# A residual adapter stack on one Trainium2 core: two batches quantised in halves, and additions moved into accumulating DMAs

## The chip, the cores and the metric

The kernel runs on one core of a Trainium2 chip. A core has five engines that run side by side and wait for each other through semaphores: TensorE (PE; PEld is its weight load), VectorE (DVE), ScalarE (ACT), GpSimd (POOL) and SyncE (SP), which here only issues transfers. The metric is the device time of one execution in microseconds; lower is better.

## The reference

`x` has 8 batches of 256 tokens with 1024 features, in float32. Four residual steps follow each other:

```
x1 = x + quantise(x; 8 thresholds, deltas, zero points)
x2 = x1 + x1 @ W1[a_b].T                 # a_b: adapter of batch b, 1024 x 1024
x3 = x2 + x2 @ W2.T + 0.5 * (x2 @ A[l_b]) @ B2.T      # rank 32
x4 = x3 + (x3 @ B3[a_b].T) @ A3[a_b].T                # rank 16
```

`quantise` counts for each element how many of the 8 thresholds are at least its absolute value; the count picks delta and zero point; x/delta is rounded, shifted, clipped to 0..63 and dequantised. Where all eight thresholds hold (the count is 8) the result is 0.

## The kernel before

All work lies transposed: 128 features in the partitions, `KT` = 8 such blocks, and `T` = 256 tokens in the columns, so a batch is a tile of 128 x 2048. `G` = 8 groups.

*Quantising.* Each batch takes 8 steps, numbered `n` from 0 over all batches (`STEPS` = 64). For a step ScalarE computes `multiple(n)` (x/delta plus a rounding constant, into the ring `tq` of 3) and `exceeds(n)` (a mask, ring of 2). VectorE computes `value(n)`, `clamp(n)` and `select(n)` (a predicated copy into `y`). At the end `close_batch` cuts and adds: `x1 = x + y`, written into `xs`, and raises `x1_ready`. Other work of the two engines is written into this sequence at fixed steps: `ACT_G` and `ACT_E` (steps at which ScalarE copies adapter tables G and E out of PSUM), `ACT_W2` and `DVE_W2` (W2's eight rows), and, counted from a batch's end, `X2_AT`, `V_AT`, `U_AT`, `LOW_AT`, `OUT_AT`.

*W1.* TensorE computes x2 = (W1 + I) x1 in float32 (`w1_x1`, two matmul passes, 64 products of 256 columns a batch). The identity is added to W1's diagonal blocks by GpSimd (`w1_diagonal`), in pairs `j` = 0 to 3 of output blocks.

*W2.* The product is made in three terms of a shorter format: x2 is split in `x2h` (ScalarE, `round_x2`) and `x2l` (VectorE, `split_x2`), W2 + I in `w2h` (ScalarE) and `w2l` (VectorE, a subtract), and `product` adds x2h w2h, x2l w2h and x2h w2l. A W2 row (128 x 1024) comes into one of `ST` = 4 stage buffers; GpSimd adds the identity (`w2_diagonal`); a buffer is loaded again when `w2l` of its row is done. Buffer 0 is `ua`, which later holds the adapter's U. W2 is prepared once and stays.

*Adapters.* Before batch 0 TensorE makes the tables G and E (`bilinear`, `adapters_g`, `adapters_e`), which go through DRAM. `v_x2` and `u_low` add the low-rank part to the accumulators.

*Order.* TensorE: adapter tables, then for each batch W1 (for batches above 0 with the `u_low` of the batch before in it), then W2 with `v_x2`. SyncE's queue, in order: first x (in two halves), tables, W1 and W2 rows as TensorE finishes G, then x of batch 1, E's stores, the other W2 rows, `load_u`; then in each batch the next W1 in four pairs, V, x of the batch after the next, and U.

Of the kernel before, what the change touches and what calls it, by code (L numbers as in the profile page):

```python
# [5 lines left out]
def quantised_residual_adapter_stack(nc, x, params, w1, w2t, w2n, b3t, b2n, b2r, a3, la, ids_b, ids_a,  # L6
# [12 lines left out]
    P = 128  # L19
# [12 lines left out]
    CP = CH // 2  # L32
# [6 lines left out]
    STEPS = B * G  # L39
# [3 lines left out]
    TQ, MK, ST = 3, 2, 4  # L43

    ctx = ExitStack()
    with ctx:
# [85 lines left out]
        w1_ready = sem("w1_ready")  # L132
# [3 lines left out]
        w2_diag = sem("w2_diag")  # L136
# [16 lines left out]
        w2l_ready = sem("w2l_ready")  # L153
# [16 lines left out]
        def _(sp):  # L170
# [69 lines left out]
            sp.wait_ge(w2l_ready, ST + 1)  # L240
# [30 lines left out]
        def _(pool):  # L271
# [39 lines left out]
        def _(act):  # L311
            def multiple(n):
                c, g = n // G, group_of(n)
                if n == 0:
                    for h in range(2):
                        act.wait_ge(x_first[h], 16)
                        nc.scalar.activation(tq[:, 0, h * CP:(h + 1) * CP], flat(xs[:, 0, h * HALF:(h + 1) * HALF, :]),
                                             ACT.Identity, bias=magic[:, 0:1], scale=rdelta[:, g:g + 1]) \
                            .then_inc(t_ready, 1)
                    return  # L320
                if n % G == 0:
                    act.wait_ge(x_in[c % 2], 16 * ((c + 1) // 2 if c % 2 else c // 2))
                if n >= TQ:
                    act.wait_ge(chosen, n - TQ + 1)
                nc.scalar.activation(tq[:, n % TQ, :], flat(xs[:, c % 2, :, :]), ACT.Identity, bias=magic[:, 0:1],  # L325
                                     scale=rdelta[:, g:g + 1]).then_inc(t_ready, 1)

            def absolute(c):
                act.wait_ge(y_cut, c)
                nc.scalar.activation(absx[:, :], flat(xs[:, c % 2, :, :]), ACT.Abs).then_inc(abs_ready, 1)  # L330

            def exceeds(n):
                if n % G:
                    act.wait_ge(abs_ready, n // G + 2)
# [5 lines left out]
                    nc.scalar.activation(mask[:, n % MK, :], absx[:, :], ACT.Relu,  # L340
# [42 lines left out]
            def tables(n):  # L383
# [19 lines left out]
            for n in range(END):  # L403
# [10 lines left out]
                for b in range(B):  # L414
                    s = n - G * (b + 1)
                    if s == V_AT + 1:
                        round_v(b)
                    for q in range(ACCS):
                        if s == OUT_AT[q] + 1 and b < LAST:
                            finish_out(b, q)  # L420
                    if s == U_AT:
                        round_u(b, 0)
                        round_u(b, 1)
                    for h, at in enumerate(X2_AT if b else X2_FIRST):
                        if s == min(at + 2, G - 1):
                            round_x2(b, h)
                    if s == LOW_AT + 1:
# [6 lines left out]
        def _(dve):  # L434
            def value(n):
                g = group_of(n)
                dve.wait_ge(t_ready, n + 2)
                nc.vector.tensor_scalar(tq[:, n % TQ, :], tq[:, n % TQ, :], -MAGIC, par[:, 1, g:g + 1],  # L438
                                        ALU.add, ALU.mult).then_inc(u_ready, 1)

            def first_value(h):
                g = group_of(0)
                dve.wait_ge(t_ready, h + 1)
                half = tq[:, 0, h * CP:(h + 1) * CP]
                nc.vector.tensor_scalar(half, half, -MAGIC, par[:, 1, g:g + 1], ALU.add, ALU.mult).then_inc(u_ready, 1)
# [12 lines left out]

            def select(n):
# [286 lines left out]
```

## Time and profile before

| | before |
|---|---|
| median of 3 runs | 491.61 us (489.53 to 491.75) |
| profiled execution, its own time | 492.2 us |
| its span | 490.4 us |
| PE busy | 457.0 us (93%) |
| DVE busy | 391.1 us (80%) |
| ACT busy | 319.7 us (65%) |
| POOL busy | 68.1 us (14%) |
| mean share of the 16 DMA engines | 36.6% |

The span runs from the first to the last instruction of the profiled execution; its own time is what the device measured for it, with what lies around the span. Busy shares are averages over stages that differ. A matmul in float32 appears as two records.

### The profile page before, as it was taken

How to read it: one execution, taken by the hardware profiler on the slowest of the kernel's cores; microseconds unless marked ns; L12 is line 12 of the kernel's file. 1: busy time of each engine (PE TensorE's matmuls, PEld its weight loads, DVE VectorE, ACT ScalarE, POOL GpSimd, SP SyncE). 2: the span in 40 equal slices, each digit the busy share in tenths (PEclk: the TensorE clock that was granted, in tenths of full speed). 3: DMA queues.
4: the chain of work that ended last, by engine and by line, in shares of the span. 5: the costliest groups of instructions: out<-in, count | busy, mean ns of one | idle time of the engine just before them, and what ended most of it. 6: DMA issues, size and time to landing. Idle time of an engine off the chain costs nothing.

```text
span 490.4 us, 5532 instructions
## 1 busy us (share of the span) xinstructions
PE 457.0 (93%) x2160; PEld 391.8 (80%) x2160; DVE 391.1 (80%) x267; ACT 319.7 (65%) x240; POOL 68.1 (14%) x46
## 2 busy tenths in 40 slices
PE   1992399997999999999999999999999999999997
PEld 1980388886888888888888888888888888888885
DVE  4997999999999999999699959995999969300100
ACT  5957899739984995697839884797569782104001
POOL 1072060380012004300020002000210002000000
PEclk9997599999999999999999999999999999999999
DMA  8997151740185018500760047201850074102002
GB/s 281 365 347 273 52 172 33 285 188 4 44 319 200 0 44 315 204 0 16 269 247 31 0 147 303 111 0 43 315 203 0 13 275 158 32 0 87 0 1 86
DMA packets 16818, 67.03 MB, mean 137 GB/s; under 512 B 2464, under 2 KB 5792, under 8 KB 11808
## 3 DMA queue, kind: packets, MB, share of 16 engines
q1 hardware_dynamic: 16800, 66.81, 36.6%
q8 instruction: 9, 0.15, 0.1%
q14 instruction: 9, 0.07, 0.0%
HBM read 56.84 MB, written 9.96 MB: 136 GB/s over the span
## 4 chain that ended last, share of the span: by engine, by line
PE 82%; DVE 11%; ACT 2%; issue 2%; DMA 1%; SPq 1%; DVEq 0%; ACTq 0%
PE x2p L610 39%; PE acc L635 31%; DVE y L463 5%; PE acc L585 3%; PE x2p L621 3%; DVE tq L451 2%; PE acc L645 2%; DVE tq L438 2%; PE acc L647 2%; DMA rows<-own_rows 1%; DVE y L471 1%; ACT tq L325 1%; ACT mask L340 1%; PE acc L573 1%; DVE w2l L511 1%
## 5 line engine op out<-in xcount | busy, mean ns | idle before, releaser
L610 PE MATMUL x2p<-xs,w1b 128*128 128x256 f32 x1024 | 225.4, 381 | 19.9 <-DVE xs L474 19.9
L610 PEld LDWEIGHTS x2p<-xs,w1b 128*128 128x128 f32 x1024 | 195.5, 191 | 48.3 <-DVE xs L474 17.8
L325 ACT ACTIVATE tq<-xs,magic,rdelta 128x2048 f32<-128x2048 f32 x63 | 131.2, 2094 | 39.0 <-DMA xs<-x 34.2
L463 DVE COPY_PREDICATED y<-mask,tq 128x2048 f32<-128x2048 int16 x56 | 143.2, 2556 | 1.9 <-ACT mask L340 0.7
L340 ACT ACTIVATE mask<-absx,negtop 128x2048 bf16<-128x2048 f32 x56 | 111.5, 1993 | 0.4 <-DVE y L463 0.4
L284 POOL TENSOR_TENSOR w1b<-w1b,eye 128x256 f32<-128x256 f32 x32 | 53.5, 1676 | 321.3 <-DMA w1b<-w 321.3
L438 DVE TENSOR_SCALAR tq<-tq,par 128x2048 f32<-128x2048 f32 x63 | 81.6, 1304 | 2.4 <-ACT tq L325 2.4
L635 PE MATMUL acc<-w2h,x2h 128*128 128x512 f32 x256 | 81.3, 396 | 0.0
L451 DVE TENSOR_SCALAR tq<-tq,ylow,yhigh 128x2048 f32<-128x2048 f32 x56 | 80.7, 1441 | 0.0
L635 PE MATMUL acc<-w2h,x2l 128*128 128x512 f32 x256 | 79.6, 390 | 0.0
L635 PE MATMUL acc<-w2l,x2h 128*128 128x512 f32 x256 | 79.5, 389 | 0.0
L479 DVE TENSOR_TENSOR x2l<-x2p,x2h 128x1024 fp32r<-128x1024 f32 x16 | 19.5, 1220 | 55.4 <-ACT x2h L345 55.4
L635 PEld LDWEIGHTS acc<-w2h,x2l 128*128 128x128 f32 x256 | 48.1, 188 | 10.2
L635 PEld LDWEIGHTS acc<-w2l,x2h 128*128 128x128 f32 x256 | 48.0, 188 | 10.2
L635 PEld LDWEIGHTS acc<-w2h,x2h 128*128 128x128 f32 x256 | 47.5, 188 | 9.4 <-DVE x2l L479 0.3
L345 ACT ACTIVATE x2h<-x2p 128x1024 fp32r<-128x1024 f32 x16 | 16.4, 1026 | 42.8 <-PE x2p L610 42.8
L381 ACT ACTIVATE outb<-acc 128x512 f32<-128x512 f32 x32 | 17.3, 593 | 37.3 <-PE acc L647 37.3
L371 ACT ACTIVATE low_hc<-x2p,lscale 128x256 fp32r<-128x256 f32 x8 | 3.8, 471 | 31.5 <-PE x2p L621 31.5
L471 DVE SCALAR_TENSOR_TENSOR y<-absx,top,y 128x2048 f32<-128x2048 f32 x8 | 19.2, 2397 | 0.3
L474 DVE TENSOR_TENSOR xs<-xs,y 128x2048 f32<-128x2048 f32 x8 | 18.3, 2292 | 0.3
L495 DVE SCALAR_TENSOR_TENSOR low_lh<-x2p,lscale,low_hc 64x256 fp32r<-64x256 f32 x8 | 3.7, 468 | 17.6 <-ACT low_lh L373 17.6
L585 PE MATMUL acc<-xs,w1b 128*128 128x128 f32 x128 | 17.7, 297 | 0.0
(59 smaller groups left out, 249.2 us busy)
## 6 DMA issues: line engine op xcount, KB each, us to landing
w1b<-w SPq DMA_DIRECT2D x32, 1024.0 KB, 6.6
xs<-x SPq DMA_DIRECT2D x7, 1024.0 KB, 6.8
out<-outb SPq DMA_DIRECT2D x14, 512.0 KB, 2.8
w1b<-w2n SPq DMA_DIRECT2D x4, 1024.0 KB, 11.3
ring<-w2t SPq DMA_DIRECT2D x6, 512.0 KB, 6.2
ua<-e_dram SPq DMA_DIRECT2D x16, 128.0 KB, 2.5
xs<-x SPq DMA_DIRECT2D x2, 512.0 KB, 5.4
ua<-w2t SPq DMA_DIRECT2D x2, 512.0 KB, 4.5
```

The source lines that it names most:

```text
L284: nc.gpsimd.tensor_tensor(diag, diag, eye[:, :].unsqueeze(1).to_broadcast([P, 2, P]), ALU.add) \
L325: nc.scalar.activation(tq[:, n % TQ, :], flat(xs[:, c % 2, :, :]), ACT.Identity, bias=magic[:, 0:1], scale=rdelta[:, g:g + 1]).then_inc(t_ ...
L340: nc.scalar.activation(mask[:, n % MK, :], absx[:, :], ACT.Relu, bias=negtop[:, g:g + 1], scale=1.0).then_inc(mask_ready, 1)
L438: nc.vector.tensor_scalar(tq[:, n % TQ, :], tq[:, n % TQ, :], -MAGIC, par[:, 1, g:g + 1], ALU.add, ALU.mult).then_inc(u_ready, 1)
L451: nc.vector.tensor_scalar(tq[:, n % TQ, :], tq[:, n % TQ, :], ylow[:, g:g + 1], yhigh[:, g:g + 1], ALU.max, ALU.min).then_inc(clamped, 1)
L463: nc.vector.copy_predicated(y[:, :], mask[:, n % MK, :].bitcast(i16), tq[:, n % TQ, :]) \
L471: nc.vector.scalar_tensor_tensor(y[:, :], absx[:, :], top[:, G - 1:G], y[:, :], ALU.is_gt, ALU.mult).then_inc(y_cut, 1)
L474: nc.vector.tensor_tensor(xc, xc, y[:, :], ALU.add).then_inc(x1_ready, 1)
L479: nc.vector.tensor_tensor(flat(x2l[:, half, :]), x2p[:, 2 * i:2 * i + 2, :].rearrange("p j n -> p (j n)"), flat(x2h[:, half, :]).bitcast(f ...
L585: last = nc.tensor.matmul(into, w2g[:, i, o * P:(o + 1) * P], b3s[:, o, :], start=False, stop=(o == OT - 1))
L610: last = nc.tensor.matmul(x2p[:, o // 2, o % 2 * T:(o % 2 + 1) * T], w1b[:, o, at:at + P], xs[:, slot, k, :], start=(o % 2 == 0 and k == 0 ...
L635: nc.tensor.matmul(acc[2 * t + h][:, :], xp[:, k, cut], w[:, k, h * DH:(h + 1) * DH], start=(k == 0 and xp is x2h and w is w2h), stop=Fals ...
```

## The change

Batches 0 and 1 are quantised as four "chains" of 1024 columns (features 0 to 511 and 512 to 1023 of each), batches 2 to 7 as one chain of 2048 each, so there are 10 chains and 80 steps. The helper names take `width(n)` and `x_part(c)` for sizes and places; `close_batch` becomes `close_chain`. TensorE multiplies the first two batches by W1 in two parts: first the products with blocks 0 to 3 of x1 for the outputs, then those with blocks 4 to 7. For batch 0 the W2 product does all terms with `w2h` first (`HIGH`), then `v_x2`, then the term with `w2l` (`LOW`).

The identities are no longer added by a GpSimd operation but by a DMA that GpSimd issues and that adds to its destination. `w2l` is no longer subtracted by VectorE: ScalarE writes the negated `w2h` into `w2l`, and a DMA of GpSimd's adds the row to it. There are five stage buffers instead of four. The steps for the other work are set anew. TensorE's loop over batches begins with batch 2.

```diff
+    CHAINS = [(b, lo, lo + HALF) for b in range(2) for lo in (0, HALF)] + [(b, 0, KT) for b in range(2, B)]
+    STEPS = len(CHAINS) * G
-    TQ, MK, ST = 3, 2, 4
+    TQ, MK, ST = 3, 2, 5
...
+        def chain_after(b):
+            return 2 * (b + 1) if b < 1 else b + 3
+        def w2l_count(k):
+            return 16 * (k // ST + 1)
...
             def load_w2(k):
                 if k >= ST:
-                    sp.wait_ge(w2l_ready, k - ST + 1)
+                    sp.wait_ge(w2l_ready[k % ST], w2l_count(k - ST))
...
                 load_w2(j)
+            load_w2(PAIRS)
...
-            sp.wait_ge(w2l_ready, ST + 1)
+            sp.wait_ge(w2l_ready[0], w2l_count(ST))
             load_u(a0)
...
-                nc.gpsimd.tensor_tensor(diag, diag, eye[:, :], ALU.add).then_inc(w2_diag, 1)
+                pool.dma_start(diag, eye[:, :], accum_op=ALU.add).then_inc(w2_diag[k % ST], 16)
+            def w2_remainder(k):
+                pool.wait_ge(w2n_ready, k + 1)
+                pool.dma_start(w2l[:, k, :].bitcast(f32), stage[k % ST], accum_op=ALU.add) \
+                    .then_inc(w2l_ready[k % ST], 16)
...
-                nc.gpsimd.tensor_tensor(diag, diag, eye[:, :].unsqueeze(1).to_broadcast([P, 2, P]), ALU.add) \
-                    .then_inc(w1_ready, 1)
+                pool.dma_start(diag, eye[:, :].unsqueeze(1).to_broadcast([P, 2, P]), accum_op=ALU.add) \
+                    .then_inc(w1_ready[j], 16)
             for j in range(PAIRS):
                 w1_diagonal(0, j)
                 w2_diagonal(j)
-            for k in range(PAIRS, KT):
+            for k in range(PAIRS, ST):
                 w2_diagonal(k)
-            with pool.Fori(1, B) as b:
+            for k in range(ST):
+                w2_remainder(k)
+            for k in range(ST, KT):
+                w2_diagonal(k)
+            for k in range(ST, KT):
+                w2_remainder(k)
+            for b in range(1, B):
...
-        DVE_D = 2
-        ACT_G, ACT_E = 5, 6
-        ACT_W2 = (9, 9, 10, 10, 12, 13, 13, 14)
-        DVE_W2 = (8, 8, 9, 9, 11, 12, 12, 13)
-        X2_FIRST, X2_AT = (2, 5), (4, G - 1)
-        V_AT, U_AT = 3, G - 1
-        LOW_AT = G + 1
-        OUT_AT = (G + 4, G + 4, G + 5, G + 5)
+        DVE_D = 4
+        ACT_G, ACT_E = 10, 12
+        ACT_W2 = (13, 13, 14, 14, 15, 25, 25, 26)
+        X2_AT = [(4, 6), (3, 5)] + [(4, G - 1)] * (B - 2)
+        V_AT = [7] + [3] * (B - 1)
+        U_AT = [13] + [G - 1] * (B - 1)
+        LOW_AT = [14] + [G + 1] * (B - 1)
+        OUT_AT = [(17, 17, 18, 18)] + [(G + 4, G + 4, G + 5, G + 5)] * (B - 1)
...
-                    act.wait_ge(w2_diag, k + 1)
+                    act.wait_ge(w2_diag[k % ST], 16 * (k // ST + 1))
                     nc.scalar.activation(w2h[:, k, :], stage[k % ST], ACT.Copy).then_inc(w2h_ready, 1)
+                    nc.scalar.activation(w2l[:, k, :], stage[k % ST], ACT.Copy, scale=-1.0).then_inc(w2n_ready, 1)
...
-                    dve.wait_ge(w2h_ready, k + 1)
-                    nc.vector.tensor_tensor(w2l[:, k, :], stage[k % ST], w2h[:, k, :].bitcast(f32),
-                                            ALU.subtract).then_inc(w2l_ready, 1)
...
+            HIGH, LOW = ((x2h, w2h), (x2l, w2h)), ((x2h, w2l),)
...
+            FRONT, BACK = range(HALF), range(HALF, KT)
+            def first_batch():
+                pe.wait_ge(x1_ready, 1)
+                w1_x1(0, 0, range(OT), first=True, parts=FRONT)
+                pe.wait_ge(x1_ready, 2)
+                w1_x1(0, 0, range(OT), parts=BACK)
+                pe.wait_ge(g_ready, 2)
+                for i, ks in enumerate((FRONT, BACK)):
+                    pe.wait_ge(x2l_ready, i + 1)
+                    for t in range(UN):
+                        for k in ks:
+                            if t == 0:
+                                pe.wait_ge(w2h_ready, k + 1)
+                            product(t, k, HIGH)
+                pe.wait_ge(vl_ready, 2)
+                v_x2()
+                for t in range(UN):
+                    for k in range(KT):
+                        if t == 0:
+                            pe.wait_ge(w2l_ready[k % ST], w2l_count(k))
+                        product(t, k, LOW)
+            def second_batch():
+                pe.wait_ge(x1_ready, 3)
+                w1_x1(1, 1, range(OT - 2), parts=FRONT)
+                pe.wait_ge(lowl_ready, 1)
+                w1_x1(1, 1, range(OT - 2, OT), parts=FRONT)
+                for q in range(ACCS):
+                    u_low(0, q)
+                pe.wait_ge(x1_ready, 4)
+                w1_x1(1, 1, range(OT), parts=BACK)
+                w2_x2(1)
```

## Rows read from the trace of the kernel before

**Rows 1.** The page, part 4: shares of the chain that ended last, by engine.
```profile
PE 82%; DVE 11%; ACT 2%; issue 2%; DMA 1%; SPq 1%; DVEq 0%; ACTq 0%
```

**Rows 2.** The chain in order of time: start us, us, what.
```profile
125.41 17.27 PE x2p L610 x80
142.68 16.37 PE acc L635 x72
159.04 1.89 PE x2p L621 x16
...
166.40 10.36 PE x2p L610 x48
```

**Rows 3.** Timeline of PE: start us, us, engine, line, operation [idle before it, releaser].
```profile
38.58 1.02 PE L598 MATMUL x2p<-outb,dmask 128*128 128x512 f32 x2
56.60 29.61 PE L610 MATMUL x2p<-xs,w1b 128*128 128x256 f32 x128 [17.00 <-DVE xs L474]
...
112.92 10.62 PE L610 MATMUL x2p<-xs,w1b 128*128 128x256 f32 x48 [2.85 <-DVE xs L474]
```

**Rows 4.** Windows of PE: stretch, us, busy (x), granted clock, DMA share, GB/s.
```profile
42.00:44.00 2.00, 0.00 (x0) 0.76 0.15 31
...
60.00:62.00 2.00, 2.00 (x10) 0.97 0.00 0
```

**Rows 5.** Timeline of DVE.
```profile
33.86 1.75 DVE L451 TENSOR_SCALAR tq<-tq,ylow,yhigh 128x2048 f32<-128x2048 f32 x1
...
121.56 1.34 DVE L451 TENSOR_SCALAR tq<-tq,ylow,yhigh 128x2048 f32<-128x2048 f32 x1
122.81 1.28 DVE L438 TENSOR_SCALAR tq<-tq,par 128x2048 f32<-128x2048 f32 x1
124.01 2.50 DVE L463 COPY_PREDICATED y<-mask,tq 128x2048 f32<-128x2048 int16 x1
126.41 1.32 DVE L451 TENSOR_SCALAR tq<-tq,ylow,yhigh 128x2048 f32<-128x2048 f32 x1
...
158.06 2.29 DVE L474 TENSOR_TENSOR xs<-xs,y 128x2048 f32<-128x2048 f32 x1
...
205.46 2.29 DVE L474 TENSOR_TENSOR xs<-xs,y 128x2048 f32<-128x2048 f32 x1
```

**Rows 6.** Groups by form, DVE: line, shapes, count, busy us, mean ns, idle before.
```profile
L463 DVE COPY_PREDICATED y<-mask,tq 128x2048 f32<-128x2048 int16 x56 | 143.2, 2556 | 1.9 <-ACT mask L340 0.7 <-issue 0.4
...
L474 DVE TENSOR_TENSOR xs<-xs,y 128x2048 f32<-128x2048 f32 x8 | 18.3, 2292 | 0.3
...
L511 DVE TENSOR_TENSOR w2l<-ring,w2h 128x1024 fp32r<-128x1024 f32 x6 | 7.2, 1224 | 0.0
...
L445 DVE TENSOR_SCALAR tq<-tq,par 128x1024 f32<-128x1024 f32 x2 | 1.4, 748 | 0.0
```

**Rows 7.** Groups by form, ACT, same columns.
```profile
L394 ACT ACTIVATE w2h<-ring 128x1024 fp32r<-128x1024 f32 x6 | 6.1, 1041 | 0.0
...
L317 ACT ACTIVATE tq<-xs,magic,rdelta 128x1024 f32<-128x1024 f32 x2 | 2.5, 1240 | 1.8 <-DMA xs<-x 1.6 <-DVE yhigh L524 0.3
```

**Rows 8.** Timeline of ACT at the E copies.
```profile
39.63 1.09 ACT L398 ACTIVATE outb<-acc 128x512 f32<-128x512 f32 x2 [1.91 <-PE x2p L598]
```

**Rows 9.** Page part 6 (count, KB each, us to landing); timelines of SP and ACT.
```profile
out<-outb SPq DMA_DIRECT2D x14, 512.0 KB, 2.8
w1b<-w2n SPq DMA_DIRECT2D x4, 1024.0 KB, 11.3
ring<-w2t SPq DMA_DIRECT2D x6, 512.0 KB, 6.2
...
91.41 0.45 SPq L172 DMA_DIRECT2D xs<-x  x1
...
105.00 4.10 ACT L325 ACTIVATE tq<-xs,magic,rdelta 128x2048 f32<-128x2048 f32 x2 [8.22 <-DMA xs<-x]
```

**Rows 10.** One line, GpSimd's W1 diagonal: ns min/median/max, first and last start.
```profile
L284 POOL TENSOR_TENSOR w1b<-w1b,eye x32: 726/1157/6553, 25.9 to 413.4; 128x256 f32<-128x256 f32 x32
```

More of the change, by code:

```diff
@@ L131, in quantised_residual_adapter_stack @@
         x1_ready = sem("x1_ready")
-        w1_ready = sem("w1_ready")
+        w1_ready = [sem(f"w1_ready{j}") for j in range(PAIRS)]
         w1_used = sem("w1_used")
@@ L135, in quantised_residual_adapter_stack @@
         out_ready = sem("out_ready")
-        w2_diag = sem("w2_diag")
+        w2_diag = [sem(f"w2_diag{c}") for c in range(ST)]
+        w2n_ready = sem("w2n_ready")
         x2h_ready = sem("x2h_ready")
@@ L152, in quantised_residual_adapter_stack @@
         w2h_ready = sem("w2h_ready")
-        w2l_ready = sem("w2l_ready")
+        w2l_ready = [sem(f"w2l_ready{c}") for c in range(ST)]
         block = ctx.enter_context(nc.Block())
@@ L545, in _ @@
                         value(n + 1)
-                for b in range(B):
-                    if n == G * (b + 1) + G - 1 and X2_AT[1] == G - 1 and b:
+                for b in range(1, B):
+                    if n - G * chain_after(b) == G - 1 == X2_AT[b][1]:
                         split_x2(b, 1)
@@ L599, in adapters_e, with w1_x1 @@
                                      a3s[:, cols], start=False, stop=True).then_inc(e_done, 1)
-            def w1_x1(b, slot, tiles, first=False):
+            def w1_x1(b, slot, tiles, first=False, parts=range(KT)):
                 for o in tiles:
-                    if o % 2 == 0:
-                        pe.wait_ge(w1_ready, PAIRS * b + o // 2 + 1)
-                    if first and o == HALF:
+                    if o % 2 == 0 and parts[0] == 0:
+                        pe.wait_ge(w1_ready[o // 2], 16 * (b + 1))
+                    if first and o == HALF and parts[0] == 0:
                         pe.wait_ge(e_ready, 2 * EH)
-                    for k in range(KT):
+                    for k in parts:
                         at = (k - o) % KT * P
@@ L613, in w1_x1 @@
                                                 skip_group_check=True)
-                    if o % 2 == 1:
+                    if o % 2 == 1 and parts[-1] == KT - 1:
                         last.then_inc(w1_used, 1)
@@ L624, in v_x2, with product @@
                 last.then_inc(low_done, 1)
-            def product(b, t, k, first=False, halves=(0, 1)):
+            HIGH, LOW = ((x2h, w2h), (x2l, w2h)), ((x2h, w2l),)
+            def product(t, k, terms=HIGH + LOW, halves=(0, 1)):
                 cut = slice(t * P, (t + 1) * P)
-                for xp, w in ((x2h, w2h), (x2l, w2h), (x2h, w2l)):
-                    if first and t == 0 and xp is x2h:
-                        if w is w2h:
-                            pe.wait_ge(w2h_ready, k + 1)
-                        else:
-                            pe.wait_ge(w2l_ready, k + 1)
+                for xp, w in terms:
                     for h in halves:
@@ L650, in _ @@
             LOW_TILES = 3
-            def batch(b, slot, first=False, last=False):
-                pe.wait_ge(x1_ready, b + 1)
-                if first:
-                    w1_x1(b, slot, range(OT), first=True)
-                    pe.wait_ge(g_ready, 2)
-                else:
-                    w1_x1(b, slot, range(LOW_TILES))
-                    for q in range(ACCS):
-                        u_low(b - 1, q)
-                    w1_x1(b, slot, range(LOW_TILES, OT))
+            FRONT, BACK = range(HALF), range(HALF, KT)
@@ new lines, in second_batch, with batch @@
+            def second_batch():
[8 more added lines that the diff above has]
+                w2_x2(1)
+            def batch(b, slot, last=False):
+                pe.wait_ge(x1_ready, b + 3)
+                w1_x1(b, slot, range(LOW_TILES))
+                for q in range(ACCS):
+                    u_low(b - 1, q)
+                w1_x1(b, slot, range(LOW_TILES, OT))
+                w2_x2(b, last)
@@ L662, in batch, with w2_x2 @@
+            def w2_x2(b, last=False):
                 pe.wait_ge(x2l_ready, 2 * b + 1)
                 for t in range(UN):
-                    if not first:
-                        pe.wait_ge(out_ready, ACCS * (b - 1) + 2 * (t + 1))
-                    for k in range(HALF):
-                        product(b, t, k, first)
+                    pe.wait_ge(out_ready, ACCS * (b - 1) + 2 * (t + 1))
+                    for k in FRONT:
+                        product(t, k)
                 pe.wait_ge(x2l_ready, 2 * b + 2)
@@ L671, in batch @@
                     v_x2()
-                    for k in range(HALF, KT):
-                        product(b, 0, k, first)
+                    for k in BACK:
+                        product(0, k)
                     u_low(b, 0)
@@ L676, in batch @@
                     for h in range(2):
-                        for k in range(HALF, KT):
-                            product(b, 1, k, first, (h,))
+                        for k in BACK:
+                            product(1, k, halves=(h,))
                         u_low(b, 2 + h)
                 else:
-                    for k in range(HALF, KT):
-                        product(b, 0, k, first)
+                    for k in BACK:
+                        product(0, k)
                     pe.wait_ge(vl_ready, 2 * (b + 1))
                     v_x2()
-                    for k in range(HALF, KT):
-                        product(b, 1, k, first)
+                    for k in BACK:
+                        product(1, k)
             bilinear()
@@ L690, in _ @@
             adapters_e()
-            batch(0, 0, first=True)
-            with pe.Fori(0, LAST // 2) as p:
-                batch(2 * p + 1, 1)
+            first_batch()
+            second_batch()
+            with pe.Fori(0, (LAST - 2) // 2) as p:
                 batch(2 * p + 2, 0)
+                batch(2 * p + 3, 1)
+            batch(LAST - 1, (LAST - 1) % 2)
             batch(LAST, LAST % 2, last=True)
```

111 lines of the change are left out of this document (49 added, 62 removed).

## The prediction

> **What bounds the kernel now.** I began with the page's chain that ended last, then read it in order of time, then each engine's timeline up to 170 us. The reader is to see that TensorE ends everything: 82% of the chain is its own [rows 1]. From 112.92 us it runs without a gap: batch 1 takes 53.5 us (112.92 to 166.40), and each later one the same [rows 2]. What is left to win is ahead of that. TensorE idles (after the first loads) twice: 17.0 us from the end of the adapter products to the first W1 product, and 2.85 us between batches 0 and 1; both are waits for VectorE's quantised x1 [rows 3]. The first of them also costs clock: idle from 39.6 us, TensorE is granted half (1.2 of 2.4 GHz) from about 43 us (0.76 over 42 to 44), and gets full clock back some 3.5 us after work resumes at 56.6, which makes that W1 product 29.3 us instead of the later 27.6 (10.36 + 17.27) [rows 2 to 4].
>
> Behind that, VectorE is the second bound: it closes batch 0 at 56.5 and batch 1 at 112.8, just ahead of TensorE's starts [rows 3], and batch 2 at 160.3 us [rows 5]. TensorE asks for batch 2 at 166.4, so VectorE is only 6.1 us ahead there; from then on it needs 47.4 us a batch (160.3 to 207.7, [rows 5]) against 53.2, and gains 5.8 each time. So the whole change comes down to one number: when can batch 2's W1 product start? It starts at 166.40 now and needs both TensorE's end of batch 1 and the third close. Everything after is 324.0 us of gapless TensorE work (490.4 - 166.4) that the change leaves alone. The profiled execution took 492.2 us, 1.8 above its span and 0.6 above the median of 491.6; I take the change of that start off the median.
>
> **The change, part by part.**
>
> *Widths.* Batches 0 and 1 now go in four half chains of 1024 columns. VectorE's durations give a fixed part: subtract 1.22 at 1024 columns, add 2.29 at 2048; value 0.75 [rows 6] against 1.28 [rows 5]. By starts, a full step is 1.25 (clamp, 121.56 to 122.81) + 1.20 (value) + 2.40 (select) = 4.85 [rows 5]. Half a step: value 0.66 (two took 1.41), clamp 0.72 by the same halving; no half select is in the trace: 1.20 if it is exactly half; with 1.07 for 1024 columns (2.29 - 1.22) the full 2.50 has a fixed 0.36, and the half would be 1.43, by starts 1.34 to 1.43. I take 1.34, since the other operations keep their fixed part too. Step 2.72, chain 8 x 0.66 + 8 x 0.72 + 7 x 1.34 + 2.4 close = 22.9 us. Four chains cost 32 x (2.72 - 2.43) = 9.4 us more than two full batches. Removed from VectorE are eight w2l subtracts of 1.14 (1.22 less the overlap of 0.08 that the adds show) = 9.1 us [rows 6]. So VectorE wins nothing in sum. On ScalarE operations overlap by 0.1; a half multiple takes 1.24 (1.14 with the overlap), one w2 copy 1.04 (0.95) [rows 7]. The half mask lies between the two; I take 1.04. The new negated copies, of the w2 copy's shape, add 8 x 0.95 = 7.6 us.
>
> *Chains 0 and 1.* Chain 0: first value about 7.0 (x's first half is in at 5.7 and one half multiple follows), then the 22.9, dmask 0.4 and small waits: closed 30.9. TensorE is with the adapters until 39.6, as before, so this half is ready long before it. Front W1 (half of 27.6) runs 39.6 to 53.5; its W1 tiles have long been on the way (GpSimd adds the first diagonal at 25.9 [rows 10]), and pair 3 is needed only at 50. Chain 1 would be closed at 54, but ScalarE stands in the way: step 12 has the four E copies, which wait for TensorE until 39.6 (a stall that is there now [rows 8]) and end 41.75; then steps 13 and 14 carry two W2 rows each: multiple 1.14 + mask 1.04 + 4 x 0.95 = 6.0 apiece; step 15 one row, 4.1; the last mask 1.04: 41.75 + 12.0 + 4.1 + 1.05 = 58.9. The masks and tq rings are two and three deep, so VectorE waits for each. Select 1.34, close 2.4: x1's second half at 62.7. TensorE idles 9.2 us (53.5 to 62.7), and back W1 ends at 76.5; with the half clock after the idle 1.6 more, 78.1 (85.9 now).
>
> *W2 products of batch 0.* Chain 2 closes at 62.7 + 22.9 + 2.3 (two x2l) + 0.65 (v_hl) + some 1.6 of waits for ScalarE's late x2h and the like = 90.2. The x2l halves come at 77.4 and 85.1, front HIGH products (7.3 us, 32 of 0.227 [rows 2]) end at 85.4, and row 4 at 86.3. Rows 5, 6, 7 of w2h stand in ScalarE's queue at steps 25 and 26, behind the Abs that waits for chain 2's close (89.1): ready at 91.0, 92.9, 97.0. That is a new stall of 9 to 10 us on TensorE, and in 11 us it works only 2.7, so I expect the half clock again: 1.7 us. From 97.0: row 7 0.9, four of t=1 3.65, v_x2 1.9, LOW 7.3: 110.8, with the clock 112.5. It ends at 110.1 now [rows 3]. The next batch starts at once instead of at 112.92: batch 1 ends 112.5 + 53.3 = 165.8. First path.
>
> *VectorE to the third close.* Chain 3: 22.9, ScalarE's rows 5 to 7 hold it 3.6, u_hl and low_lh 1.7: 90.2 to 118.8 (TensorE wants it at 126, no wait). Batch 2 needs x(2). SP loads it after load_u(a0), which now waits for the remainder DMA of row 5: issued on GpSimd when the negated copy is done (91.9). Queued behind it on SP: four u, four W1, two v loads and x(2). The trace shows no accumulating DMA. Nearest rows: 512 KB take 2.8 (a store from SBUF) or 6.2 (a W2 load), and 1 MB in the crowd at the start 11.3 [rows 9]; I keep 2.8 and 11.3 as ends. I take 5, nearer the loads, since the queues are empty but it reads both operands: lands 97, u 2.2, W1 issues 2.5 (x(2) goes out 101.9; 91.4 now), and 13.6 to land as now (91.41 to 105.0): 115.5. ScalarE gives the first multiple at 117.7, the first mask at 125.5, and VectorE is back in step 0.7 late. Third close: 118.8 + 47.5 (112.8 to 160.3) + 0.7 - 1.5 for GpSimd operations that no longer stretch VectorE's = 165.5. Second path.
>
> *Diagonals by DMA.* In batches 1 to 7 they land perhaps 2 to 7 us later than GpSimd's add of 0.7 to 6.6; W1 loads of a later batch go out 20 us and more ahead of use, so this costs nothing; without that cover each would cost its lateness four times a batch. For batch 1, pair 0 lands about 108, wanted at 112: free too. GpSimd's own operations go; a clamp of VectorE's beside them took 1.75 instead of 1.34 [rows 5], but up to 113 us that lies mostly where VectorE will wait for ScalarE anyway. This is where a rule could speak against the change: GpSimd's 128x256 add takes 0.73 to 6.55 us [rows 10], so the two engines do hold each other up. The Trainium skill, SBUF — State Buffer, section "SBUF: two separate sides", says a DMA issued from GpSimd can't get its descriptors written while VectorE holds the shared port pair, and gives 3.1 instead of 0.62 us. By that rule (no DMA of GpSimd's is in this trace to agree or not) each issue would pay it, and the sum would be case C's below.
>
> Sum: batch 2 starts at the later of 165.8 and 165.5, plus 0.1: 165.9, against 166.4. Gain 0.5 us: 491.1.
>
> **The rivals.**
>
> *A, halves cost half (faster).* If select and mask have little fixed part, chains 2 and 3 take 2.2 us less each: w2h rows, x(2) and both paths come 2 to 3 us earlier, and if the clock is not lost 1.7 more: start 161.5 to 163.5, 486.5 to 489. For it: VectorE's fixed part at 2048 is only known from other operations. Against: the E copies pin ScalarE's pile to 39.65 us, and halves of value and multiple do keep their fixed part.
>
> *B, the remainder DMA is slow (slower).* SP's queue hangs on row 5's remainder. Every us over 5 puts x(2) and the third close back by one; it decides (over 2.5 us slower) from 8.5 us on. At 11.3, the crowded end, the third close is 171.8: 497.4. For it: read, add and write of 512 KB. Against: at 92 us the queues are empty.
>
> *C, GpSimd can't issue in time (slower).* Nine DMAs stand in its queue before the first remainder, and ScalarE's row 4 wants its diagonal at 56. From 25.9 that leaves 2.8 us an issue; if each takes 4 (inside the 0.73 to 6.55 that GpSimd's add takes beside VectorE [rows 10]), row 4 comes at 67, x1's second half and all after it 9 to 11 us later: about 500. The Trainium skill's rule in SBUF — State Buffer, above, would bring this about.
>
> *D, the full gain (faster).* TensorE's 17.0 + 2.85 idle and 1.7 us of clock all go and nothing takes their place: 21 us. I exclude it but for 0.03: VectorE was only 6.1 us ahead at the third close, so more than 6 can't be had unless its chains shrink; the cap is 485.5.
>
> **How the numbers follow.** Forecast 0.42, A 0.27, D's cap 0.03, B 0.19, C 0.09. A measurement of this kernel can tell about 0.5% (2.5 us) from no change. Faster 0.30, within 0.42, slower 0.28. Both signs hold much, so the range goes from 485.5 (cap) to 497 (B's end, C left out); the likeliest case's own range is 489.2 to 494.
>
> **What would show it.** Right: first W1 product at 39.7; a TensorE gap of about 9 us near 54 to 63, released by VectorE's x1; a gap near 86 to 97 released by ScalarE's w2h; batch 2's first product near 166; VectorE gaps for ScalarE at 40 to 60. Half selects at 1.3 to 1.4. A: half selects near 1.25, the close of chain 2 before 88. B: x(2)'s landing after 118 and ScalarE waiting for it. C: GpSimd's DMA issues of 4 us, ScalarE waiting for w2_diag before 56 us. The prediction is wrong if batch 2's first product isn't between 164 and 168.5, or if gaps open after it.

## The result, and the profile after

| | before | changed kernel |
|---|---|---|
| median | 491.21 us (4 runs) | 515.41 us (4 runs) |
| ratio to before | | 1.0484, 95% interval 1.0433 to 1.0535 |
| span of the profiled execution | 490.4 us | 512.8 us |
| batch 2's first W1 product | 166.40 us | 188.42 us |

One of the four timed executions of the changed kernel took 1684.05 us; the median counts it and the ratio leaves it out (the median of the other three is 514.54 us), and it stays unexplained.

The change is 4.8% slower. I had forecast 491.1 us, no measurable change, and 485.5 to 497 as the range. The span grew by 22.4 us and the start of batch 2 came 22.0 us later, so the loss lies where I had said that all of it would be decided, ahead of batch 2. From the page of the changed kernel come its shares of the chain that ended last and two rows of its transfers (count, KB each, us to landing). `w1b<-eye` is the DMA that adds the identity to a W1 diagonal, `w2l<-ring` the one that adds a W2 row to its negated copy (the remainder):

```profile
PE 69%; DMA 8%; DVE 8%; issue 7%; ACT 6%; SPq 2%; POOL 1%; ACTq 0%; DVEq 0%
...
w1b<-eye POOLq DMA_DIRECT2D x32, 128.0 KB, 4.1
...
w2l<-ring POOLq DMA_DIRECT2D x6, 512.0 KB, 8.3
```

TensorE had 82% of the chain [rows 1]; now transfers, and time in which no wait is shown, have taken their part. TensorE's timeline of the changed kernel, its groups with a gap before them (start, length, and in brackets the gap and its releaser):

```profile
57.86 6.44 PE L619 MATMUL x2p<-xs,w1b 128*128 128x256 f32 x16 [5.52 <-DMA w1b<-eye]
69.32 16.20 PE L619 MATMUL x2p<-xs,w1b 128*128 128x256 f32 x64 [5.02 <-DVE xs L496]
97.10 0.87 PE L641 MATMUL acc<-w2h,x2h 128*128 128x512 f32 x2 [3.37 <-ACT w2h L420]
...
126.80 16.46 PE L619 MATMUL x2p<-xs,w1b 128*128 128x256 f32 x64 [8.18 <-DMA w1b<-eye]
...
188.42 10.62 PE L619 MATMUL x2p<-xs,w1b 128*128 128x256 f32 x48 [1.64 <-DVE xs L496]
```

Against [rows 3]: the 17.0 us gap became several. The one for x1's second half is there, but it ends at 69.3 instead of my 62.7. Two gaps that I hadn't forecast wait for a W1 diagonal: pair 3 of batch 0 (5.5 us, until 57.9) and pair 0 of batch 1 (8.2 us, until 126.8). GpSimd's timeline shows what led to the first (its last row is from batch 1):

```profile
26.26 1.33 POOL L307 DMA_DIRECT2D w1b<-eye  x1 [23.68 <-DMA w1b<-w]
...
37.11 1.39 POOL L307 DMA_DIRECT2D w1b<-eye  x1 [8.58 <-issue]
...
44.84 1.39 POOL L307 DMA_DIRECT2D w1b<-eye  x1 [4.93 <-issue]
...
48.90 1.20 POOL L307 DMA_DIRECT2D w1b<-eye  x1 [1.73 <-issue]
53.73 0.91 POOL L296 DMA_DIRECT2D ring<-eye  x1 [3.63 <-issue]
58.12 0.87 POOL L296 DMA_DIRECT2D ring<-eye  x1 [3.48 <-issue]
...
127.00 1.22 POOL L307 DMA_DIRECT2D w1b<-eye  x1 [10.49 <-issue]
```

In these rows an issue itself takes 0.9 to 1.4 us. But GpSimd stands still ahead of it, "issue" being time for which the profile shows no wait: 8.6 us before pair 1, though its load had landed at 32.1. ScalarE asked for W2's rows in the meantime. Its timeline in the changed kernel:

```profile
53.48 1.06 ACT L420 ACTIVATE w2h<-ring 128x1024 fp32r<-128x1024 f32 x1 [3.74 <-DMA ring<-eye]
...
58.19 1.06 ACT L420 ACTIVATE w2h<-ring 128x1024 fp32r<-128x1024 f32 x1 [2.70 <-DMA ring<-eye]
...
143.82 1.09 ACT L407 ACTIVATE outb<-acc 128x512 f32<-128x512 f32 x2 [7.06 <-PE acc L653]
```

The first two rows are 6.4 us of waits in ScalarE's pile of copies, and x1's second half came 6.6 us later than worked out. The third comes back below. The chain in order of time shows the second transfer gap:

```profile
98.40 4.49 DMA w2l<-ua
...
103.10 0.35 SPq L201
...
105.64 1.33 SPq L212
...
107.83 0.83 SPq L213
...
110.05 4.83 DMA w1b<-w
114.88 0.44 issue
115.31 11.35 DMA w1b<-eye
126.66 0.14 issue
126.80 16.46 PE x2p L619 x64
```

The remainder of W2's row 5 lands in 4.5 us, near the 5 that I took. Then SP sends U (L201) and reads batch 1's adapter numbers (L212 and L213), and W1's pair 0 goes out only at 110.05, 7.2 us after that landing. Pair 0's diagonal, 128 KB, takes 11.4 us. It lands at 126.7, and GpSimd's next issue starts at 127.0 (the last row of its timeline).

### The profile page after: what moved, and what is told of

It is laid out like the page before. It is cut to its first block, busy times and chain, and to the rows that moved or that the text cites. A ratio compares the mean times of both kernels' runs of the same rounds, so it can differ in the third digit from the quotient of the medians.

```text
span 512.8 us, 5602 instructions
## 1 busy us (share of the span) xinstructions
PE 467.8 (91%) x2160; PEld 396.8 (77%) x2160; DVE 378.2 (74%) x307; ACT 335.5 (65%) x279; POOL 71.0 (14%) x54
## 4 chain that ended last, share of the span: by engine, by line
PE 69%; DMA 8%; DVE 8%; issue 7%; ACT 6%; SPq 2%; POOL 1%; ACTq 0%; DVEq 0%
PE x2p L619 36%; PE acc L641 26%; DVE y L485 3%; DMA w1b<-w 2%; DMA w1b<-eye 2%; PE x2p L630 2%; ACT mask L366 2%; PE acc L594 2%; PE acc L651 1%; DMA rows<-own_rows 1%; PE acc L653 1%; DVE tq L466 1%; DVE tq L473 1%; ACT tq L351 1%; DVE y L493 1%
## 5 line engine op out<-in xcount | busy, mean ns | idle before, releaser
L619 PE MATMUL x2p<-xs,w1b 128*128 128x256 f32 x1024 | 231.9, 388 | 22.2 <-DMA w1b<-eye 15.6
L351 ACT ACTIVATE tq<-xs,magic,rdelta 128x2048 f32<-128x2048 f32 (+1 forms) x80 | 139.3, 1750 | 39.7 <-DMA xs<-x 30.9
L485 DVE COPY_PREDICATED y<-mask,tq 128x2048 f32<-128x2048 int16 (+1 forms) x70 | 142.7, 2038 | 8.2 <-ACT mask L366 7.1
L366 ACT ACTIVATE mask<-absx,negtop 128x2048 bf16<-128x2048 f32 (+1 forms) x70 | 115.6, 1651 | 2.5 <-DVE y L485 2.5
L466 DVE TENSOR_SCALAR tq<-tq,par 128x2048 f32<-128x2048 f32 (+1 forms) x80 | 85.4, 1076 | 28.6 <-ACT tq L351 28.6
L307 POOL DMA_DIRECT2D w1b<-eye x32 | 53.9, 1685 | 327.6 <-DMA w1b<-w 221.2
L473 DVE TENSOR_SCALAR tq<-tq,ylow,yhigh 128x2048 f32<-128x2048 f32 (+1 forms) x70 | 79.3, 1133 | 0.0
L371 ACT ACTIVATE x2h<-x2p 128x1024 fp32r<-128x1024 f32 x16 | 16.4, 1023 | 37.5 <-PE x2p L619 37.5
L356 ACT ACTIVATE absx<-xs 128x2048 f32<-128x2048 f32 (+1 forms) x9 | 14.6, 1620 | 11.9 <-DVE y L493 11.9
L493 DVE SCALAR_TENSOR_TENSOR y<-absx,top,y 128x2048 f32<-128x2048 f32 (+1 forms) x10 | 19.3, 1926 | 0.3
L496 DVE TENSOR_TENSOR xs<-xs,y 128x2048 f32<-128x2048 f32 (+1 forms) x10 | 18.7, 1865 | 0.3
## 6 DMA issues: line engine op xcount, KB each, us to landing
w1b<-w2n SPq DMA_DIRECT2D x4, 1024.0 KB, 11.2
```

The source lines that it names most:

```text
L307: pool.dma_start(diag, eye[:, :].unsqueeze(1).to_broadcast([P, 2, P]), accum_op=ALU.add) \
L351: nc.scalar.activation(tq[:, n % TQ, 0:width(n)], x_part(c), ACT.Identity, bias=magic[:, 0:1], scale=rdelta[:, g:g + 1]).then_inc(t_ready, 1)
L366: nc.scalar.activation(mask[:, n % MK, 0:width(n)], absx[:, 0:width(n)], ACT.Relu, bias=negtop[:, g:g + 1], scale=1.0).then_inc(mask_ready, 1)
L466: nc.vector.tensor_scalar(v, v, -MAGIC, par[:, 1, g:g + 1], ALU.add, ALU.mult).then_inc(u_ready, 1)
L473: nc.vector.tensor_scalar(v, v, ylow[:, g:g + 1], yhigh[:, g:g + 1], ALU.max, ALU.min) \
L485: nc.vector.copy_predicated(y[:, 0:width(n)], mask[:, n % MK, 0:width(n)].bitcast(i16), tq[:, n % TQ, 0:width(n)]).then_inc(chosen, 1)
```

## The experiments

Each ratio is to the kernel before on the same chip, with its 95% interval. "Batch 2" is the start of its first W1 product; 166.40 us before.

| run | us | ratio | batch 2 |
|---|---|---|---|
| changed kernel | 515.41 | 1.0484 (1.0433 to 1.0535) | 188.42 |
| e4_scratch: 2.5 times the descriptor memory | 506.71 | 1.0301 (1.0265 to 1.0337) | 180.10 |
| e1_w1_add: W1's diagonals by GpSimd | 498.81 | 1.0150 (1.0118 to 1.0181) | 172.13 |
| e2_diag_add: e1, and W2's diagonals too | 499.80 | 1.0165 (1.0136 to 1.0195) | 173.28 |
| e12_neg_copies: e3, with ScalarE's negated copies as dead work | 498.22 | 1.0127 (1.0101 to 1.0152) | 172.37 |
| e3_halves: the halves alone | 493.88 | 1.0042 (1.0026 to 1.0058) | 167.73 |
| e5_before_w1dma: before, W1's diagonals by DMA | 490.22 | 0.9973 (0.9959 to 0.9988) | 164.58 |
| e6_sp_order: twice the descriptor memory, U loaded later | 499.92 | 1.0174 (1.0153 to 1.0196) | 174.51 |
| e7_halves_sp: e3, U loaded later | 494.07 | 1.0056 (1.0035 to 1.0077) | 167.34 |
| e8_halves_rows: e7, W2's rows early | 492.47 | 1.0020 (1.0006 to 1.0033) | 165.78 |
| e9_first_only: e8, batch 0 alone in halves | 495.46 | 1.0078 (1.0053 to 1.0104) | 169.43 |
| e10_pair0_alone: twice the descriptor memory, pair 0 sent alone | 512.1 (one run) | | 186.00 |
| e11_first_w1dma: e9, W1's later diagonals by DMA | 495.33 | 1.0074 (1.0046 to 1.0103) | 170.24 |

**One part of the transfers undone at a time.** e1:

```diff
-                pool.dma_start(diag, eye..., accum_op=ALU.add).then_inc(w1_ready[j], 16)
+                nc.gpsimd.tensor_tensor(diag, diag, eye..., ALU.add).then_inc(w1_ready[j], 1)
```

> The changed kernel with one part undone: W1's diagonals are again added by a GpSimd operation; W2's diagonals and remainders stay accumulating DMAs. Theory T (the transfers: W1's diagonal DMAs land late and fill GpSimd's queue, so the DMAs behind them go out late): the TensorE waits for w1b<-eye (15.6 us) go, W2's diagonals of rows 2 and 3 land before ScalarE asks (53.5 and 58.2 now), x1's second half comes near 63 instead of 69.3; about 500 us (496 to 504). Rival S (the halves and ScalarE's pile of copies are what costs, the DMAs only fill the gaps): 510 or more.

It measured 498.8: both gaps for w1b<-eye are gone, and x1's second half comes at 61.3. TensorE's timeline of e1:

```profile
61.32 15.71 PE L619 MATMUL x2p<-xs,w1b 128*128 128x256 f32 x64 [9.31 <-DVE xs L496]
...
172.13 10.62 PE L619 MATMUL x2p<-xs,w1b 128*128 128x256 f32 x48 [1.73 <-DVE xs L496]
```

The gap of 9.3 us up to 61.3 is the one that I had worked out as 9.2 up to 62.7. So W1's diagonals carry 16 of the 24 us; the rival (the structure costs) expected 510 or more.

e2 puts W2's diagonals back as well:

```diff
-                pool.dma_start(diag, eye[:, :], accum_op=ALU.add).then_inc(w2_diag[k % ST], 16)
+                nc.gpsimd.tensor_tensor(diag, diag, eye[:, :], ALU.add).then_inc(w2_diag[k % ST], 1)
```

> Both kinds of diagonals again by GpSimd operations, only the remainders of W2 stay accumulating DMAs. T: x1's second half near 62.7 as I had worked out, batch 2's first W1 product near 168; 492 to 497 us. S: within 2 us of the kernel with only W1's diagonals undone, and over 505.

It measured 499.8, above the 492 to 497 that T gave; W2's diagonals alone cost nothing once W1's are out of GpSimd's queue. What was left over the kernel before, 7.6 us, wasn't in them, so e3 took the remainders away:

```diff
-                    nc.scalar.activation(w2l[:, k, :], stage[k % ST], ACT.Copy, scale=-1.0).then_inc(w2n_ready, 1)
...
-                pool.dma_start(w2l[:, k, :].bitcast(f32), stage[k % ST], accum_op=ALU.add)
...
+                    dve.wait_ge(w2h_ready, k + 1)
+                    nc.vector.tensor_tensor(w2l[:, k, :], stage[k % ST], w2h[:, k, :].bitcast(f32), ALU.subtract)
```

> Only the halves and the five stage buffers are left of the change: no accumulating DMA, w2l by VectorE's subtract at steps 12, 12, 13, 13, 14, 24, 24, 25, no negated copies on ScalarE. T: ScalarE's pile is 3.8 us shorter a pair of rows, x1's second half near 60, SP is freed for x(2) before 100; 486 to 491 us, that is no slower than before. S: over 500, since the half chains cost VectorE 9.4 us and nothing gives them back.

It measured 493.9 us, ratio 1.0042: 2.9 us above the top of what I had expected (486 to 491) and far under the rival's 500. What is left of the change, the halves with the fifth stage buffer and TensorE's new order, costs 0.4%. The remainders and their copies cost 5.9 us, and it was open whether by ScalarE or by the transfer. e12 is e3 with the negated copies as dead work, overwritten by the subtract:

```diff
+                    nc.scalar.activation(w2l[:, k, :], stage[k % ST], ACT.Copy, scale=-1.0).then_inc(w2n_ready, 1)
...
+                    dve.wait_ge(w2n_ready, k + 1)
```

> The halves alone (no accumulating DMA) with the eight negated copies put back on ScalarE as dead work: they are written into w2l, and VectorE's subtract overwrites them after. The remainders by DMA cost 5.9 us over the halves alone (499.8 against 493.9). If that is ScalarE's extra 7.6 us of copies in its pile: 497.5 to 500. If it is the remainder DMA's landing, on which SP's queue waits before it loads U, W1 and x(2): 493.5 to 496.

498.2, inside the range for ScalarE: 4.3 of the 5.9 us are its copies (their order ahead of the subtracts included). The other 1.6 us are the transfer's net of VectorE's eight subtracts, which e12 does and e2 doesn't; the intervals of e12 and e2 overlap, so they aren't clear of noise. TensorE's timeline of e12:

```profile
63.69 15.73 PE L617 MATMUL x2p<-xs,w1b 128*128 128x256 f32 x64 [10.50 <-DVE xs L487]
...
172.37 10.62 PE L617 MATMUL x2p<-xs,w1b 128*128 128x256 f32 x48 [1.70 <-DVE xs L487]
```

In e3 these stand at 60.98 and 167.73. The first 2.7 us are lost in ScalarE's pile of copies at steps 13 to 15, the other 1.9 behind it.

**Why W1's diagonals cost.** e4 is the whole change with more memory for GpSimd's descriptors:

```diff
-    dynamic_dma_scratch_size=1024
+    dynamic_dma_scratch_size=2560
...
-        b2s = sb("b2s", [P, KT, R2])
+        b2s = va
```

> The whole change as it is, with the memory for the descriptors of GpSimd's DMAs doubled (1024 to 2048 bytes a partition; the adapter tile b2s shares va's place to make room). Theory T1 (GpSimd's gaps before an issue are waits for room: an earlier DMA must have landed): the gaps of 5 to 10 us before the second issue of a burst shrink, x1's second half comes by 3 us or more earlier, 503 to 510 us. Rival T2 (the gaps come from VectorE holding the memory port, or the landing of each DMA is slow in a crowd): no change, 514 to 516.

The kernel of this run has 2560 bytes a partition, 2.5 times the 1024, and not the 2048 that its expectation names; e6 and e10 below have the 2048. It measured 506.7, inside T1's range. GpSimd's timeline of e4:

```profile
31.16 1.26 POOL L307 DMA_DIRECT2D w1b<-eye  x1 [2.45 <-DMA w1b<-w]
...
35.81 1.20 POOL L307 DMA_DIRECT2D w1b<-eye  x1 [2.09 <-DMA w1b<-w]
...
40.52 1.22 POOL L307 DMA_DIRECT2D w1b<-eye  x1 [1.67 <-DMA w1b<-w]
```

Pair 1 goes out at 31.2 instead of 37.1, pair 3 at 40.5 instead of 48.9, each right behind its load. The same instructions beside the same VectorE work have no "issue" gaps, so these were waits for room, not for VectorE's port. `b2s` in `va`'s place, the other part of the edit, isn't what removes them: e6 and e10 have it too, and still some gaps. Ahead of the 32 W1 diagonals the "issue" gaps come to 106.3 us (24 of them) with 1024 bytes, 16.1 us (4) in e6 and 8.8 us (2) in e10 with 2048, and none with 2560. What is left of this part is pair 0 of batch 1; the chain of e4:

```profile
102.25 4.68 DMA w1b<-w
106.93 0.44 issue
107.37 11.01 DMA w1b<-eye
118.51 16.32 PE x2p L619 x64
```

Room doesn't help here: 11.0 us. In e10, the whole change with 2048 bytes, SP holds the next loads until this DMA has landed:

```diff
                 for j in range(PAIRS):
+                    if b == 0 and j == 1:
+                        sp.wait_ge(w1_ready[0], 32)
```

> The whole change with the doubled descriptor memory, and SP doesn't send W1's pairs 1 to 3 and x(2) of batch 1 before pair 0's diagonal DMA has landed. If that DMA's 11 us (107.4 to 118.5 in the run with the doubled memory) is the crowd of 1 MB loads that go out right behind its own load: it lands in 3 to 5 us, TensorE's 7.2 us wait for pair 0 shrinks below 2, and the rest of the loads and x(2) come 3 to 5 us later; 500 to 507 us. If an accumulating DMA of this form is slow by itself there: again 9 us or more to land, and over 508.

The chain of e10:

```profile
107.70 3.17 DMA w1b<-eye
...
111.05 4.74 DMA w1b<-w
115.78 0.49 issue
116.27 10.80 DMA w1b<-eye
127.07 0.04 issue
127.11 8.07 PE x2p L621 x22
```

Pair 0's diagonal lands in 3.17 us when nothing is behind it, against 11.01. Pair 1's, which now has the crowd (two pairs and x(2), 3 MB) behind it, takes 10.80. The DMA engines moved 41 GB/s during the first and 334 GB/s during the second. VectorE was busy 3.1 of the first 3.2 us and 1.1 of the later 10.8, so its port isn't what delays the landing. The crowd is the cause, shown on the same instruction twice. The time, 512.1 from one run, missed my 500 to 507: I had not seen that the delay would move to pair 1, and TensorE waited 12.4 us for it.

e5 asks whether such a DMA costs wherever it stands:

```diff
 (kernel before)
-                nc.gpsimd.tensor_tensor(diag, diag, eye..., ALU.add).then_inc(w1_ready, 1)
+                pool.dma_start(diag, eye..., accum_op=ALU.add).then_inc(w1_ready[j], 16)
```

> The kernel before with one part of the change alone: W1's diagonals (all batches) added by accumulating DMAs, everything else as before. Theory T (the diagonal DMA itself is only late by 4 to 12 us; it costs because the changed kernel loads W1 of batch 1 at 110 instead of 88 us and wants pair 3 of batch 0 early): here TensorE asks for batch 0's tiles at 56.6 and for batch 1's at 112.9, and pair 0 goes out near 93, so most is hidden: 491 to 496 us. Rival (each diagonal by DMA costs by itself, whatever its place): 500 or more.

It is the one run that beats the kernel before, by 0.27%, and is also faster than the 491 to 496 that I had expected. Three rows of it, from TensorE's timeline, VectorE's groups by form and GpSimd's line:

```profile
111.12 10.62 PE L610 MATMUL x2p<-xs,w1b 128*128 128x256 f32 x48 [0.65 <-DVE xs L474]
```
```profile
L451 DVE TENSOR_SCALAR tq<-tq,ylow,yhigh 128x2048 f32<-128x2048 f32 x56 | 75.6, 1350 | 0.0
```
```profile
L284 POOL DMA_DIRECT2D w1b<-eye x32: 1209/1218/2747, 26.1 to 417.0; - x32
```

Batch 1 starts 1.8 us earlier than in [rows 3], and VectorE's clamps take 1.35 us on the mean instead of 1.44: with W1's additions gone from GpSimd they are stretched less. The diagonals are as late as in the changed kernel (3.2 to 11.2 us to land), but nobody waits: batch 1's W1 goes out at 88 us and is wanted at 111.

**SP's order, and how tight the halves are.** e6 (the whole change with 2048 bytes) and e7 (on e3) load batch 0's U behind batch 1's W1 and x(2):

```diff
-            sp.wait_ge(e_out, 16 * EH)
-            sp.wait_ge(w2l_ready[0], w2l_count(ST))
-            load_u(a0)
...
                     load_x(b + 2)
+                if b == 0:
+                    sp.wait_ge(e_out, 16 * EH)
+                    sp.wait_ge(w2l_ready[0], w2l_count(ST))
+                    load_u(a0)
```

> The whole change with the doubled descriptor memory, and SP's order changed: batch 0's U (which waits for row 5's remainder) is loaded behind batch 1's W1 and x of batch 2, no longer ahead of them. Theory (the two remaining losses, pair 0's diagonal at batch 1 and x of batch 2, come from loads that stand behind that wait in SP's queue): W1's first pairs go out near 78 instead of 102, x(2) near 91 instead of 105; the 7.2 us wait for pair 0 goes, the third close comes at 163 to 166 instead of 180; 491 to 495 us. Rival (the diagonals' landing in a crowd costs wherever the loads are): 502 or more.

499.9: 6.8 us better than e4 (with less descriptor memory than e4), but 5 above the top of what I expected. The wait for pair 0 went. In its place the remainder of the last W2 rows fell into the crowd (the chain has `97.82 10.54 DMA w2l<-ring`, which was 4.5 for row 5 alone before), and U's load, behind the crowd, kept ScalarE 6.8 us. The crowd moves; it doesn't go away.

> The halves alone (no accumulating DMA) with the same change of SP's order. If x of batch 2 at 113 us is what makes VectorE late there (x2l waits of TensorE of 2.3 + 2.3 us in batch 1, third close 167.6): 488.5 to 491 us. If ScalarE's and VectorE's own queues set it: 493 to 494, as with the halves alone.

494.1, at the 493 to 494 expected if the queues set it, and the third close (VectorE's end of batch 2's x1) at 167.2: x(2) went out 12 us earlier than in e3 and nothing came of it. The chain of e7 says why:

```profile
108.31 13.81 PE x2p L616 x64
122.69 0.43 ACT outb L399
```

ScalarE's copies of batch 0's output stand in its queue at steps 34 and 35, and wait for TensorE's u_low, which comes after batch 1's front W1. So TensorE's lateness goes to ScalarE, from there to VectorE's fifth chain, and comes back as the third close. This is read from the chain; no run moves these copies.

e8 adds the rows 5 to 7 at steps 18 to 20:

```diff
-        ACT_W2 = (13, 13, 14, 14, 15, 25, 25, 26)
-        DVE_W2 = (12, 12, 13, 13, 14, 24, 24, 25)
+        ACT_W2 = (13, 13, 14, 14, 15, 18, 19, 20)
+        DVE_W2 = (12, 12, 13, 13, 14, 17, 18, 19)
```

> The same, and rows 5 to 7 of w2h copied at ScalarE's steps 18, 19, 20 (w2l subtracted at 17, 18, 19) instead of 25, 25, 26, so that they no longer stand behind chain 2's close. My prediction's step said that this wait costs TensorE some 9 us with the clock; the trace of the halves alone shows 4.4 us of waits and a half-speed start. If it stays on the path to batch 2: 484 to 487 us. If VectorE's third close takes over as bound: 487 to 490.

492.5, above both of my ranges (484 to 487, 487 to 490): the waits for w2h go, but with them only 1.6 us of the time. TensorE's timeline of e8:

```profile
137.54 1.22 PE L638 MATMUL acc<-w2h,x2h 128*128 128x512 f32 x2 [5.37 <-DVE x2l L492]
...
165.78 10.62 PE L616 MATMUL x2p<-xs,w1b 128*128 128x256 f32 x48 [1.61 <-DVE xs L487]
```

The time won is waited for again, now for VectorE. e9 gives VectorE its half of the halves' price back, with batch 1 as one chain (and, not shown, the steps and TensorE's loop of the kernel before for it):

```diff
-    CHAINS = [(b, lo, lo + HALF) for b in range(2) for lo in (0, HALF)] + [(b, 0, KT) for b in range(2, B)]
+    CHAINS = [(0, lo, lo + HALF) for lo in (0, HALF)] + [(b, 0, KT) for b in range(1, B)]
```

> No accumulating DMA, SP's order and the early rows as in the last experiment, but only batch 0 in halves; batch 1 is one chain of 2048 columns with the steps that the kernel before uses. Half chains cost VectorE 9.4 us in my working, half of it for batch 1, and the last run's third close (165.7 us) was what TensorE waited for. If VectorE's own work is the bound left there: third close near 160 to 162, batch 2's W1 starts at 163 to 165, 487 to 490 us. If ScalarE's wait for batch 0's output copies sets the third close, nothing is won: 491 to 493.

Rows of e9, from TensorE's and VectorE's timelines:

```profile
114.29 12.30 PE L616 MATMUL x2p<-xs,w1b 128*128 128x256 f32 x48 [11.17 <-DVE xs L487]
```
```profile
159.47 2.29 DVE L487 TENSOR_TENSOR xs<-xs,y 128x2048 f32<-128x2048 f32 x1
```

The third close comes at 161.8, inside the 160 to 162 that I expected. But batch 1, whole, closes at 114.1, TensorE stands 11.2 us for it, batch 2 starts at 169.4, and the time is 495.5, above both of my ranges. 

> Like the run with only batch 0 in halves, and W1's diagonals of batches 1 to 7 by accumulating DMA (batch 0's by GpSimd operations). In the kernel before this part alone made 0.3%: VectorE's operations weren't stretched by GpSimd's, batch 1 closed 1.8 us earlier. If that holds here too: 0.5 to 2 us below the run without it. If the late landings cost: above it.

 With W1's later diagonals by DMA it is 495.3, no difference (I had expected 0.5 to 2 us less): TensorE still stands 11.3 us for batch 1's close.

## Why the prediction was wrong, point by point

**Where all is decided** (batch 2's start, 324 us behind it): right. The start moved by 22.0, the span by 22.4 us.

**Widths:** right. A half select takes 1.33 us (28 of them, the changed kernel), and a half step in VectorE's timeline goes by in 2.59 against my 2.72. With the transfers taken out (e3), batch 2 starts at 167.7 against the 165.9 forecast for the whole, and the time is 1.0042 of before.

**ScalarE's pile and the two gaps of TensorE:** right in place where W1's diagonals are out of it, and the first also in size: x1's second half at 61.3 to 62.2 in e1 and e2 (62.7 forecast), the gap 9.3 us (9.2). The waits for w2h near 88 to 96 us were 5.9 and 6.3 us, a third less than the 9 to 10 forecast, and TensorE began batch 1 at 110.7 in e1 (112.5 forecast). Two costs were too small in it: the negated copies, which I put into the pile, cost 4.3 us to the end (e12), while I let the whole change break even. And in the changed kernel the pile also held the late diagonals.

**"Its W1 tiles have long been on the way, and pair 3 is needed only at 50":** this step failed. Pair 3's diagonal was there at 57.9. I had reckoned each issue and landing by itself, and not that with 1024 bytes of descriptor memory GpSimd's next issue waits for room; behind pair 0 of batch 1 it waited until that DMA had landed (126.7 and 127.0 above). e4 prices it: from 1.0484 to 1.0301, some 9 us, of which 7.6 are there at x1's second half (61.8 instead of 69.3). Case C had the place (GpSimd's queue, row 4 late at 67; it came at 62.3) with 0.09; its cause, VectorE's port, isn't what held it here. The Trainium skill, SBUF — State Buffer, section "SBUF: two separate sides", has VectorE keep GpSimd from writing descriptors while it holds the shared port pair, and so would let it hold up each issue. The traces don't agree for these instructions: in e5 an issue takes 1.2 us at the median, and from 56 to 111 us VectorE is busy 54.9 of 55 us beside them.

**"For batch 1, pair 0 lands about 108, wanted at 112: free too":** this step failed, and it is the larger error of sizing. It landed at 126.7, wanted at 118.6. My 108 left the diagonal some 4 us. It took 11.0 to 11.4, because 4 MB of loads (three pairs and x(2)) go out right behind its own; alone it takes 3.2 (e10). From e4 to e1 that is 1.0301 to 1.0150, some 7.5 us. Its load was late too: it went out at 110.05, against some 99.2 by my sum. The remainder landed 5.9 us later than I had it, and SP then took 7.2 us to the W1 load instead of 2.2, because I had left out the reading of the adapter numbers (in the chain above). SP's timeline of the kernel before had this term: 5.9 us from U at 82.33 to W1 at 88.19. No run prices it by itself. My bounds for a DMA reached to 11.3, but I put them on the remainder alone, whose 5 was right (4.49), and let the diagonals off for their cover. The Trainium skill, DMA: Bandwidth & Descriptors, section "Anatomy of one DMA — SWDGE (gpsimd) path", gives 2.0 us and the bytes at 436 GB/s, for 128 KB an estimate of 2.3; the 3.2 alone is 0.9 us above it, the 11 isn't in the formula.

**"VectorE to the third close" as a path of its own:** this step failed. I worked out two paths to batch 2, 165.8 and 165.5, and took the later. They aren't two: ScalarE's output copies of batch 0 tie VectorE's fifth chain to TensorE's progress in batch 1 (the 7.06 us row of the changed kernel, the chain of e7). A late pair 0 counts on both. The third close moved from my 165.5 to 188.3, 22.8 us: x(2) was there 11.5 us later than I had it, and 7.1 us more are this wait of ScalarE's. The tie is read from the chains and not tested by itself. The sum of this path also had two small slips: its parts to the end of chain 3 make 118.4 and not 118.8, and case B's end is 497.1 and not 497.4; neither changes the forecast.

**The rivals:** A (halves cost half) didn't come; nor did D, and e8 and e9 show why its 21 us can't be had: as soon as TensorE's waits go, VectorE's take their place. B priced the wrong DMA: the remainder landed in 4.5 us. Its sign came all the same (ScalarE waited 8.2 us for x(2), until 127.0), by the later copies and SP's time, so that sign didn't single B out.

In shares, from the ratios in turn (in another order of undoing they could differ): the halves 0.4%, ScalarE's negated copies 0.85%, the remainders' transfer 0.4%, W2's diagonals nothing (-0.15%, inside the intervals), W1's diagonals in the crowd 1.5%, the room for descriptors 1.8%.

## What to carry to other kernels

Before moving a small addition from an engine into a DMA, ask what goes out right behind the load that it waits for: its time to land is that of the crowd, not its own, and it is hidden only where the load is sent a crowd's length ahead of use, as in e5 (88 against 111 us) and not in the changed one (110 against 119). Count how many such DMAs may be under way at once, too. And when two engines both look just in time, look for the instruction that ties them, here an output copy in ScalarE's queue, before adding up their paths as if each ran alone.

## What the runs showed of the hardware that I had not expected

GpSimd's stream stood still for up to 10.5 us ahead of an accumulating DMA with 1024 bytes of descriptor memory a partition; with 2560 bytes these gaps were gone (e4: none in the whole trace; 8.7 us of the time), with 2048 a few of up to 5.4 us were left (e6, e10). And a 128 KB accumulating DMA took 3.2 us alone and 10.8 to 11.4 us with 3 to 4 MB of plain loads issued behind it. The same operation on GpSimd takes 0.7 to 6.6 us [rows 10], but lengthens VectorE's beside it, so that where it is hidden the DMA is the better of the two by 0.3% (e5).
